# Third and fourth weight pair of layer 1: turned by VectorE from exchanged 32-wide blocks instead of transposed by TensorE

## The reference, cut to what matters

```python
xn = _layernorm(x)
s = recurrent part of layer 1: y = (xn @ W_in.T) * k, k = sum_s(B_real*C_real - B_imag*C_imag)
    s = xn + rmsnorm(y @ W_out.T) * norm_w
hidden = fwht(silu(xn @ W1.T) * (xn @ W3.T))      # W1, W3: (1024, 256)
g = silu(hidden @ W2.T)                            # W2: (256, 1024)
x = x + s * g
# layer 2: causal attention with qkv, o_proj, gamma, beta, and the same feed-forward with its own W1, W2, W3
```

## Time and profile before

| | |
|---|---|
| median of 3 runs | 357.87 us (357.84 to 357.94) |
| profiled execution, own time | 357.93 us |
| its span in the trace | 356.1 us |
| PE busy | 350.6 us, 98% |
| DVE busy | 248.8 us, 70% |
| ACT busy | 167.5 us, 47% |
| POOL busy | 105.2 us, 30% |
| TensorE clock granted | full over the span |

### The profile page before, as it was taken

The page is one execution under the profiler, slowest core; times in us unless marked ns, Lnnn a source line. Parts: engine busy times, 40 slices in busy tenths (PEclk is TensorE's granted clock), DMA queues, the critical chain, the costliest instruction groups (busy, mean ns, idle before and its releaser), DMA issues.

```text
span 356.1 us, 4969 instructions
## 1 busy us (share of the span) xinstructions
PE 350.6 (98%) x1785; PEld 297.9 (84%) x1785; DVE 248.8 (70%) x482; ACT 167.5 (47%) x326; POOL 105.2 (30%) x122
## 2 busy tenths in 40 slices
PE   7999999999999999999999999999999999999996
PEld 4887888888888888888988879888888888888896
DVE  5679964995499667956498874887547886356645
ACT  2865442446254724363465634654346544464510
POOL 2164410456036934662024030240300603004000
PEclk9999999999999999999999999999999999999999
DMA  7999679215150303130351302606014251054001
GB/s 244 242 188 229 157 111 123 64 40 129 53 129 17 111 12 106 35 117 0 120 148 39 112 0 83 179 18 197 2 59 147 62 159 49 14 177 130 5 3 59
DMA packets 69648, 34.44 MB, mean 97 GB/s; under 512 B 40692, under 2 KB 69624, under 8 KB 69624
## 3 DMA queue, kind: packets, MB, share of 16 engines
q1 hardware_dynamic: 69480, 34.06, 37.9%
q10 hardware_dynamic: 144, 0.07, 0.1%
HBM read 21.99 MB, written 12.12 MB: 96 GB/s over the span
## 4 chain that ended last, share of the span: by engine, by line
PE 96%; DVE 2%; DMA 1%; POOL 0%; issue 0%; ACT 0%
PE GU L358 20%; PE GU L360 20%; PE GU L359 20%; PE O L358 8%; PE O L359 8%; PE O L360 8%; PE O L426 1%; PE T L358 1%; DMA X<-in_L_attn_x 1%; PE T L360 1%; PE T L359 1%; PE O L509 1%; PE O L508 1%; PE O L507 1%; PE T L365 1%; PE O L365 1%
## 5 line engine op out<-in xcount | busy, mean ns | idle before, releaser
L722 ACT ACTIVATE hf<-GU 128x512 f32<-128x512 f32 x64 | 38.2, 599 | 80.5 <-DVE hid L842 63.0
L998 DVE TENSOR_TENSOR hf<-hf,GU 128x512 f32<-128x512 f32 x64 | 43.5, 679 | 30.0 <-PE GU L360 24.1
L842 DVE TENSOR_TENSOR hid<-hf,hid 128x512 fp32r<-128x512 f32 x64 | 51.2, 801 | 0.3
L358 PE MATMUL GU<-XT,W1T 128*128 128x512 f32 x128 | 50.5, 395 | 0.0
L360 PE MATMUL GU<-XT,W1T 128*128 128x512 f32 x128 | 49.9, 390 | 0.0
L359 PE MATMUL GU<-XT,W1T 128*128 128x512 f32 x128 | 49.9, 390 | 0.0
L358 PE MATMUL GU<-XT,W3T 128*128 128x512 f32 x128 | 49.8, 389 | 0.0
L360 PE MATMUL GU<-XT,W3T 128*128 128x512 f32 x128 | 49.8, 389 | 0.0
L359 PE MATMUL GU<-XT,W3T 128*128 128x512 f32 x128 | 49.8, 389 | 0.0
L358 PE MATMUL O<-hid,W2hi 128*128 128x512 f32 x112 | 43.9, 392 | 0.0
L359 PE MATMUL O<-hid,W2hi 128*128 128x512 f32 x112 | 43.7, 390 | 0.0
(11 more groups left out here) (205 smaller groups left out, 729.8 us busy)
## 6 DMA issues: line engine op xcount, KB each, us to landing
swap_rows<-GX SPq DMA_DIRECT2D x7, 512.0 KB, 3.3
sT<-swap_rows SPq DMA_DIRECT2D x28, 128.0 KB, 2.7
swap_gate<-GX SPq DMA_DIRECT2D x7, 512.0 KB, 2.9
sT<-swap_gate SPq DMA_DIRECT2D x28, 128.0 KB, 2.7
stage<-in_L_ffn_W SPq DMA_DIRECT2D x12, 256.0 KB, 4.3
swap_p<-PX SPq DMA_DIRECT2D x4, 640.0 KB, 3.2
PL<-swap_p SPq DMA_DIRECT2D x16, 160.0 KB, 3.1
stage<-in_L_ffn_W SPq DMA_DIRECT2D x32, 64.0 KB, 2.6
```

Source lines behind the costliest of these rows:

```text
L358: pe.matmul(o, lhs(0), rhs(0), start=start, stop=False)
L722: act.activation(hf[:, c % 2, :], GU[:, c % 2, 0, :], ACT.Silu).then_inc(silu_done, 1)
L842: dve.tensor_tensor(dst, src, hi_part.bitcast(F32), ALU.subtract).then_inc(done, 1)
L998: dve.tensor_tensor(hf[:, c % 2, :], hf[:, c % 2, :], GU[:, c % 2, 1, :], ALU.mult).then_inc(mul_done, 1)
```

## The change

W1 and W3 of pairs 2 and 3 are no longer transposed by PE. SP loads each by `load_blocks` (four DMAs of 64 KB with 128-byte runs instead of one of 256 KB), DVE turns it in place (`first_turn`), ACT takes the hi part from `stage` (`first_turned_hi`), and POOL the lo part (`first_pair_lo`). W2 of these pairs is still loaded as before and transposed by PE. The loads and small operations stand in another order:

- SP: the five small tensors of k (`ssm`) go first, then pair 2, the second group's x, pair 3, and only then W_in, W_out and qkv; norm_w, gamma and beta follow qkv.
- DVE: `first_turn(2)` stands ahead of chunk 1, `first_turn(3)` ahead of chunk 3, `k_vector` behind `nat_lo(3)`; four `pair_lo` operations are gone.
- ACT: the scaling of W_in stands behind chunk 5 instead of ahead of chunk 4; the identity is loaded after a wait for DVE's first memset.
- PE: the transpose of gamma and beta goes to group 1 (bank T).
- POOL: four lo parts are new, and ahead of `pair_butterfly(0, 3, 4)` stands a wait for the normalised rows of group 1 (`xn_ready` 3).

```diff
+            def load_first_blocks(i, w):
+                sp.wait_ge(w_tr, 2 * (i - 2) + w + 1)
+                load_blocks(stage[:, i % 2, w, :], (W1, W3)[w][0][2 * P * i:2 * P * (i + 1), :], stage_loaded[i % 2][w])
@@ SP's stream
-            sp.dma_start(X[:, TILES:2 * TILES, :], xt_dram[:, TILES:2 * TILES, :]).then_inc(xnext_loaded, 16)
-            sp.wait_ge(w2_tr, 1)
-            load_pair(0, 2, stage[:, 0, :, :], stage_loaded[0])
             for i, m in enumerate((A_theta, B_real, B_imag, C_real, C_imag)):
                 sp.dma_start(ssm[:, i, :, :], m.rearrange("c (a p) s -> p (c a) s", p=P)).then_inc(kv_loaded, 16)
+            load_first_blocks(2, 0)
+            sp.wait_ge(w2_tr, 1)
+            load_first_w2(2)
+            load_first_blocks(2, 1)
+            sp.dma_start(X[:, TILES:2 * TILES, :], xt_dram[:, TILES:2 * TILES, :]).then_inc(xnext_loaded, 16)
+            sp.wait_ge(w2_tr, 2)
+            load_first_w2(3)
+            load_first_blocks(3, 0)
+            load_first_blocks(3, 1)
             sp.dma_start(win[:, :, :], W_in.rearrange("(a p) k -> p a k", p=P)).then_inc(win_loaded, 16)
...
-            sp.wait_ge(w2_tr, PAIRS - 1)
+            sp.wait_ge(hx_lo, 2)
             load_w(PAIRS)
@@ PE
-                head_pair(2)
                 head_pair_w2(2)
...
-                head_pair(3)
                 head_pair_w2(3)
...
-                small_natural()
@@ PE up_chunk
+                if first and c in (4, 6):
+                    pe.wait_ge(hx_lo, c - 2)
@@ ACT
+            def first_turned_hi(i):
+                for w, WT in enumerate((W1T[0], W3T[0])):
+                    hi(WT[:, 0, :, 2 * P * i:2 * P * (i + 1)], stage[:, i % 2, w, :].rearrange("p (k h) -> p k h", k=KC),
+                       hx_turned, 2 * (i - 2) + w + 1, hx_hi)
@@ DVE
+            def first_turn(i):
+                for w in (0, 1):
+                    dve.wait_ge(stage_loaded[i % 2][w], landed(i))
+                    in_place(stage[:, i % 2, w, :]).then_inc(hx_turned, 1)
...
+                first_turn(2)
                 chunk(0, 1)
-                pair_lo(0, 2, 2)
                 nat_lo(2, w2nat)
                 chunk(0, 2)
+                first_turn(3)
+                chunk(0, 3)
+                nat_lo(3, w2nat)
                 k_vector()
-                chunk(0, 3)
                 dve.wait_ge(xnext_loaded, 16)
-                pair_lo(0, 3, 3)
-                nat_lo(3, w2nat)
                 stats(1, TILES)
@@ POOL
+            def first_pair_lo(i):
+                for w, WT in enumerate((W1T[0], W3T[0])):
+                    pool.wait_ge(hx_hi, 2 * (i - 2) + w + 1)
+                    pool.tensor_tensor(WT[:, 1, :, ...], stage[:, i % 2, w, :], WT[:, 0, :, ...], ALU.subtract).then_inc(hx_lo, 1)
...
                 pair_butterfly(0, 0, 1)
+                first_pair_lo(2)
                 pair_butterfly(0, 1, 2)
                 quad_butterfly(0, 0, 4)
+                first_pair_lo(3)
                 pair_butterfly(0, 2, 3)
                 rstd_of(1)
+                pool.wait_ge(xn_ready, 3)
                 pair_butterfly(0, 3, 4)
```

More of the change, by code:

```diff
@@ L299, in _ @@
             load_pair(0, 1, stage[:, 1, :, :], stage_loaded[1])
-            sp.dma_start(X[:, TILES:2 * TILES, :], xt_dram[:, TILES:2 * TILES, :]).then_inc(xnext_loaded, 16)
-            sp.wait_ge(w2_tr, 1)
-            load_pair(0, 2, stage[:, 0, :, :], stage_loaded[0])
             for i, m in enumerate((A_theta, B_real, B_imag, C_real, C_imag)):
                 sp.dma_start(ssm[:, i, :, :], m.rearrange("c (a p) s -> p (c a) s", p=P)).then_inc(kv_loaded, 16)
-            sp.dma_start(win[:, :, :], W_in.rearrange("(a p) k -> p a k", p=P)).then_inc(kv_loaded, 16)
+            load_first_blocks(2, 0)
[7 more added lines that the diff above has]
+            load_first_blocks(3, 1)
+            sp.dma_start(win[:, :, :], W_in.rearrange("(a p) k -> p a k", p=P)).then_inc(win_loaded, 16)
             load_blocks(woutT[:, :, :].rearrange("p m d -> p (m d)"), W_out, wout_loaded)
-            sp.wait_ge(w2_tr, 2)
-            load_pair(0, 3, stage[:, 1, :, :], stage_loaded[1])
+            load_blocks(wqkvT[:, :, :, :].rearrange("p w c d -> p (w c d)"), qkv, wqkv_loaded)
             sp.dma_start(normB[:, :], norm_w.rearrange("(a d) -> a d", a=1).broadcast_to([P, D])).then_inc(small_loaded, 16)
@@ L315, in _ @@
             sp.dma_start(mask[:, :], consts[:, 2, :]).then_inc(mask_loaded, 16)
-            sp.wait_ge(w2_tr, PAIRS - 1)
+            sp.wait_ge(hx_lo, 2)
             load_w(PAIRS)
             move_rows(1)
-            sp.wait_ge(w2_tr, PAIRS)
+            sp.wait_ge(hx_lo, 4)
             load_w(PAIRS + 1)
@@ L410, in head_hadamard, with small_gb @@
                 pair_hadamard(i, w2nat)
-            def small_natural():
+            def small_gb():
                 pe.wait_ge(small_loaded, 16 * N_SMALL)
-                pe.wait_ge(w2nat_ready, PAIRS)
-                pe.transpose(O[:, 0, 0:2 * KC], gbrow[:, :], ident[0:2 * KC, 0:2 * KC]).then_inc(gb_tr, 1)
+                pe.transpose(T[:, 0, 0:2 * KC], gbrow[:, :], ident[0:2 * KC, 0:2 * KC]).then_inc(gb_tr, 1)
             def small_m():
@@ L457, in up_chunk @@
                     pe.wait_ge(xt_ready, 2 * n + 2)
-                if first and c % 2 == 0:
-                    pe.wait_ge(w_lo, c + 2)
+                if first and c == 2:
+                    pe.wait_ge(w_lo, 4)
+                if first and c in (4, 6):
+                    pe.wait_ge(hx_lo, c - 2)
                 if c >= 2:
@@ L564, in block0_group @@
                     up_chunk(0, n, c, False)
+                    if c == 1 and n == 1:
+                        small_gb()
                     if c == 1 and n > 1:
@@ L750, in block0_head @@
                 chunk(0, 3, True)
+                first_turned_hi(3)
                 pair_u(0, 2, 2)
-                pair_hi(0, 3, 3)
                 nat_hi(3, w2nat)
+                chunk(0, 4, True)
+                chunk(0, 5, True)
+                pair_u(0, 3, 3)
+                act.wait_ge(win_loaded, 16)
                 act.wait_ge(kvec_ready, 1)
@@ L778, in block0_group @@
                     chunk(n, c, False)
+                    if c == 2 and n == 1:
+                        hi(gb[:, :, :].rearrange("p g k -> p (g k)"), T[:, 0, 0:2 * KC], gb_tr, 1, gb_ready)
                     if c == 2 and n > 1:
```

25 lines of the change are left out of this document (14 added, 11 removed).

## The result

The changed kernel takes 362.91 us (median of 4 runs, 362.79 to 363.44), the kernel before 357.90 (357.84 to 358.36). The ratio is 1.0141, 95% interval 1.0126 to 1.0156: 5.0 us slower, where 1.4 were forecast. The direction was right, the size was not, and 362.91 lies above the range.

The account below looks back on a forecast made before the run. PE bounds the kernel, with DVE's chain 0.3 us behind; pair 3's late landing outweighs PE's 1.8 us gain: 357.93 + 1.4, less 0.06, gives 359.3 us; range 356.4 to 360.8, likeliest case 358.4 to 360.3.

Parts of the forecast that it names:

- What bounds it: Head: PE 98% busy, but DVE's chain arrives beside it at group 0's first down chunk, with 0.3 us of slack.
- Rival (b): Head: PE's whole gain from the dropped transposes is kept, 356.1 us; chance 0.14.
- (a): SP's stream: blocks come without stops, chunk 4 at 28.85 to 29.15, PE gains 0.5 to 0.8, 357.2 us; chance 0.25.
- What comes off PE: Pairs 2 and 3: eight transposes each go, 1.74 us; with small gaps 1.8 us as PE's own gain.
- When it lands: SP's queue: pair 3's last block load lands at 25.1 us, from issue costs, stops and landing, between 23.2 and 27.
- L: Landing time of pair 3's last block load: 25.1 us, between 23.2 and 27.
- T: End of pair 3's second turn on DVE: L + 0.65, 25.75 us.
- From the landing to PE: DVE's chain behind T: chunk 4's product at 31.05, VR's lo part ends 48.8, first down matmul 48.85, +1.4 us.
- The hidden lo part: Chunk 3's lo part on DVE, slowed beside POOL's lo part of W3 of pair 3: +0.3 us.
- Behind it: Behind chunk 4: everything keeps its spacing; PE waits ahead of chunk 6, `small_m` and the first down chunk.
- The edits costed at nothing: ACT's identity wait, gamma and beta's moved transpose, POOL's four lo parts (6 us, in idle time): each costs nothing.
- Rival (c): Group 1's gate product waits for its late gather, PE loses 1.5 us more, 361 us; chance 0.11.

Follow-up runs that it names:

- e10: Changed kernel with plain loads of pairs 2 and 3 and GpSimd's four lo parts shortened to 8 of 256 columns: 358.28 us, ratio 1.0006.
- e1: Changed kernel without ACT's wait ahead of the identity's load: 362.84 us, ratio 1.0140.
- e4: Changed kernel with one GpSimd butterfly, pair_butterfly(0, 2, 3), behind the computation of rstd instead of ahead: 363.80 us, ratio 1.0154.
- e5: Changed kernel with layer 2's second block load of W1 and W3 behind the first gate's move on SP: 363.00 us, ratio 1.0138.
- e11: Changed kernel, block loads kept, with only GpSimd's four lo parts shortened to 8 of 256 columns: 362.20 us, ratio 1.0106.
- e2: Changed kernel with the five small tensors of k behind pair 3's blocks instead of ahead of pair 2's: 362.69 us, ratio 1.0136.
- e9: Changed kernel with plain loads of pairs 2 and 3 instead of block loads, GpSimd's lo parts whole: 359.60 us, ratio 1.0040.
- e6: Changed kernel with DVE's k ahead of pair 3's turns and layer 2's second block load behind the first gate's move: 361.08 us, ratio 1.0083.
- e3: Changed kernel with DVE's five operations of k ahead of the turns of pair 3: 363.68 us, ratio 1.0183.

## Why the prediction was right in kind and wrong in size

- **What bounds it.** Right, and stronger than put. Two chains arrive side by side at the first down chunk; in e10, with block loads and GpSimd's lo parts out of the way, the shorter PE chain brings the first down matmul forward by 0.07 us and the time by nothing (358.28 against 358.15 us; the moved transpose takes 0.4 of it). Rival (b), 356.1, was not to be had; (a), with 0.5 to 0.8 us gained, was too hopeful as well, because DVE's chunk 4 stood at 29.58 and not at 28.85 to 29.15 even there. The statement that no gap is left in DVE's stream is a little too strong: it waits 0.5 and 0.2 us for ACT behind chunk 4, in both kernels.
- **What comes off PE.** 1.74 us, right as work: 16 matmuls less, with waits of about the same length in their place (e10).
- **When it lands: the step that failed.** The mechanism was right, the term L was mis-sized. L was put at 25.1 us, between 23.2 and 27; in the profiled execution it came at 27.7 (the turn released at 27.69), over the upper end, and at 26.0 to 26.8 in e1, e4, e5 and e11: too low by 0.9 to 2.6 us. By terms, in the profiled execution: the five small tensors took 5.4 us of SyncE's queue (5.29 to 10.69), where 2.9 plus 0.6 stood in the sum. Their price of 0.57 us came from the earlier trace rows, a place with 768 KB issued in the 1.4 us ahead of it; here 1.5 MB of pair loads stand in front and they cost 0.85 to 1.32 (in the other kernels that have them here the first costs 0.47 to 0.58, the last three 0.9 to 1.5, all five 4.4 to 5.1). That this is the place and not the tensors, e2 shows: there four of the five cost 0.51 to 0.62 (the fifth 1.68). The first eight block DMAs took 5.4 us and the last eight 6.36, with one stop, less than I had allowed (5.64, and 5.64 + 1.3). So the last issue began at 23.79 instead of 22.5. Its landing took 3.9 us instead of the 2.6 of the earlier trace rows. Why is open: x of group 1 and the W2 part had landed by 20.7 and 21.8, before it was issued, and the last two loads of pair 3 took 2.5 to 4.0 us in e1, e4, e5 and e11. 1.3 us each from issue and landing is the 2.6 by which T was late (28.3 against 25.75). e9, with those loads plain, gives 3.3 us back. (The 140 GB/s of the earlier trace rows is not the rate of 128-byte runs alone, since o_proj and a part of x were issued at 27.53 and 28.93, in or just ahead of that stretch; the sum does not use it.)
- **From the landing to PE.** 5.3 us predicted, 6.3 measured. The hidden lo part, which I had slowed beside GpSimd, ran free (0.68 us), because W3's hi part on ACT released GpSimd only at 29.14; k, which I had left alone, was slowed, 2.0 us instead of 1.0. The mechanism was named, at the wrong instruction. With the landing this is 3.6 us too little: chunk 4's product at 34.62, not 31.05. Where the landing is earlier (e1), k is still slowed and chunk 4's product is at 33.21.
- **Behind it.** Right: VR's lo part is 17.04 us after chunk 4's product in both kernels, and 0.3 us of slack was used. PE waits ahead of chunk 6, but 2.97 us. The spacing behind the first down matmul, expected as before, is half a microsecond longer. No wait stands ahead of `small_m` and the down chunk in this run, because the clock's lower level had made PE late by as much; in e1, at full clock, both are there (0.79 for W_in's scaling, 0.34 for VR's lo part), at the same time.
- **The edits costed at nothing.** ACT's wait for the identity: nothing in the time (e1). The transpose of gamma and beta that "only moves to group 1": about 0.4 us, since the head, where it stood, has waits to hide it now and group 1 has none. GpSimd's four lo parts "fit in its idle time": true of GpSimd, wrong of the kernel; 0.7 to 1.3 us through DVE.
- **Rival (c), the gate.** Not active in the profiled execution of the changed kernel, where DVE is late enough itself (73.46, no wait), though U2's load ends at 62.4, behind the 60.5 from which it was to decide. It is the next limit: 1.38 to 2.27 us of wait in e1, e2, e3 and e11, lifted in e6. As e1 shows, it takes over as soon as the landing is 1.4 us earlier, so in other executions of the changed kernel it may be active; they have no trace.

## What to carry to other kernels

An engine that is 98% busy may still have no microsecond to give: where a second in-order engine arrives beside it with 0.3 us of slack, shortening the first turns into waits. A small instruction moved out of the place where it will be hidden, into one where it is not, costs its length and the gaps around it. Price a DMA's issue and landing by a row with the same bytes queued in front of it, and look at more than one execution: the landing here moved by 1.7 us between kernels with the same stream ahead of it. Work moved to an idle GpSimd is not free if VectorE has short operations beside it, and it also moves what stood behind it in GpSimd's own stream; and when a limit is removed and the time stays, look for the next one before giving up the theory, since two edits that each give nothing (e3, e5) can give 1.8 us together (e6).

## What was not expected of the hardware

- The same 32 KB loads cost 0.51 to 0.62 us of SyncE's queue in e2 (four of five; the fifth met a stop, 1.68) and 0.85 to 1.32 us behind the pair loads in the changed kernel (0.47 to 1.49 in the others); a block DMA of 64 KB was issued in 0.6 us, or 1.68 at a stop.
- VectorE's 128x64 operations rose from 0.22 to up to 1.33 us beside GpSimd, about the length of the GpSimd instruction, and a 128x512 lo part from 0.68 to 2.44 us. The product `hf<-hf,GU` (its second input in PSUM) did not: in the changed kernel it took 0.65 us at 19.52, with a GpSimd lo part running from 19.11 to 20.41.
- The granted clock fell to its lower level behind PE's wait of 2.97 us and in e5 behind one of 2.94 us, and, in e1, not behind one of 2.96 us. What told them apart is open; it cost nothing here, since DVE and ACT set the time.
- The variants scatter more than the kernel before: up to 4 us between the four runs of e2 and e3, against 0.5 us for before on that chip. e6, with the gate out of the way, has 0.8. That the gate's wait is what scatters was not tested by itself, and it is not all: e5, with the gate out of the way too, has 1.9 us between its runs.
